# Value products moved behind the next score pair, and eight steps moved to other slots, in a two-layer attention and FFN kernel

## The chip, the cores and the metric

The kernel runs on one core of one Trainium2 chip, in one launch. The metric is the device time in microseconds, as the median of several runs. In the text TensorE (PE), VectorE (DVE), ScalarE (ACT), GpSimd (POOL) and SyncE (SP) are the engines; PEld is TensorE's weight load.

## What is computed

The input x has 16 batches of 512 tokens with 128 features, in float32. There are two layers. Each one normalizes its input (layer norm without weights) and adds an attention and an FFN, both taken from the same normalized input:

```python
xn = _layernorm(x, axis=-1)
x = x + _L0_attn_ref(xn, ...) + _L0_ffn_ref(xn, ...)
xn = _layernorm(x, axis=-1)
x = x + _L1_attn_ref(xn, ...) + _L1_ffn_ref(xn, ...)
```

Layer 0's attention has 16 heads of size 8: rotary positions, causal scores with a learned bias within 64 positions, softmax, and then `relu(probs + tau/row)`, which is nonzero in the future as well where tau is positive, and multiplies the values and Wo. Layer 0's FFN (128 to 352 and back) rounds its inputs, its hidden values and its weights to FP4 in blocks of 16. Layer 1's attention is linear and causal (elu + 1 of queries and keys, a running state of key times value, a denominator). Layer 1's FFN has four experts with a router that takes the best two, and a shared one (128 to 344 and back); the kernel computes all five for every token.

## The kernel before

A batch is handled whole, as four tiles of 128 tokens (T = 4). The work is laid out by hand in **slots**: a frame f has 64 slots (SLOTS, 16 heads times four query tiles), and in frame f slot s three batches are worked on at once. Batch f has its layer-0 scores there. Batch f+1 is being prepared at position p = s, batch f is also at position p = 64 + s (ATT = 64), batch f-1 is at p = 128 + s (L1 = 128, its layer 1), and f-2 at p = 192 + s, where the last down product ends. Frames go from -1 to 16, with 8 more slots behind. The tables of positions at the top (lines 58 to 77) say in which slot each step is issued. All engines walk through the same slots, each with its own order inside a slot; what one engine needs of another it waits for with a semaphore (lines 278 to 326). So the order on an engine is fixed by the slots, and the class Schedule (lines 96 to 151) counts the tickets of the PSUM banks in the same order.

**Scores and probabilities.** A step of four slots is one group of four heads (HG = 4) with one query tile i, whose scores have (i+1) x 128 columns. In an even slot TensorE issues the scores of this slot and the next one (`scores`, line 1073; 32 rows of float16, so one quarter of the array's rows), in two PSUM banks in turn. VectorE adds the bias and takes the maximum (`biased`, 534), ScalarE the exponential and its sum (`exp_with_sum`, 915), VectorE the reciprocal of the sums at each step's end (`row_rcp_of`, 541), GpSimd scales and adds tau in the next step (`scale_probs`, 808). Two steps after the scores, in even slots, TensorE transposes these probabilities by blocks of 128 x 128 for four heads (`turn_probs`, 1084; up to two blocks in a slot, one per turn bank), ScalarE copies them with the relu into one of four buffers pb (`store_probs`, 918), and TensorE multiplies the values by them (`pv`, 1094; weights of 32 columns, the four heads side by side in the array, 8 matmul instructions a block). Once a group's last block is done, ScalarE copies its output (`store_o`, 926).

The value products of an even slot s are issued in slot s+3 (`blocks_before`, 149), on TensorE behind the extra products and the transposes. Per frame there are 40 blocks, in 24 slots. TensorE's order in a slot is: scores of the pair, extra products into the score banks (`into_scores`, 1109), transposes, value products, and the rest (`beside`, 1235).

**Extras in the score banks** (EXTRAS, line 77; all at odd slots): fx, fv and fy are the three products for the future part of layer 0's attention (a suffix sum of xn, its values, their output), kv is layer 1's state, lin its 16 key-by-query products, tot the sum of its parts. The same two banks serve them and the scores, so each waits until VectorE has taken the last but one.

**Turn banks** (TURNS, line 75): two more banks take everything that is transposed: x, its FP4 form xq, the operand stacks of both attentions (`stack`, 1063, of queries and keys as float16 parts), the hidden values, and `intra` (1210), layer 1's products of values by lin, again with 32-column weights.

**Beside them**: `qkv` (QKV0, QKV1), gate and up products (GATE0, GATE1) with ScalarE's tanh and VectorE's two products (`silu`, 586, `hidden`, 593); the FP4 rounding of the hidden values: `hidden_amax` (671), `hidden_step` (HID_STEP, 676 and 678), GpSimd's scaling (HID_SCALED), `hidden_magic` (HID_MAGIC, 433 and 435 through `fp4_magic`), GpSimd's add, subtract and multiply; the down product of layer 0 with attention's output (WO); the norm of layer 1; the router (ROUTER, sixteen small VectorE steps, two a slot, and one exponential on ScalarE); and for each of five experts the down product (DOWN1, four slots, `down1`, 1220) and its weighted addition (`accumulate`, 651, four VectorE instructions of line 661, 667 for the shared one).

VectorE's order in a slot is: the two `biased`, the extras (`from_scores`, 548), `products`, `urgent` (norms, rope, elu), the stack's copy, the reciprocal, `beside`.

## Time and profile before

| | us |
|---|---|
| median of 3 runs | 2374.54 (2372.79 to 2376.23) |
| the profiled execution | 2369.53 |
| its span | 2367.7 |
| TensorE busy, whole span | 2128.1 (90%) |
| VectorE, ScalarE, GpSimd busy | 1642.7, 1384.6, 1157.8 |
| chain that ended last | PE 59%, DVE 19%, ACT 12%, issue 7%, POOL 2% |
| mean granted TensorE clock | 0.971 |

The busy time of TensorE is no measure of its speed: matmuls are pipelined and their ends are modelled, so that the distances between starts say more than durations. A row of the timeline merges equal neighbours: its start is that of the first, its count stands behind the x, and where two rows follow each other on TensorE, the difference of their starts is what the first one really took.

### The profile page before, as it was taken

To read this page: it belongs to the slowest core of one execution; us is meant where nothing else is said; L and a number is where in the kernel's file an instruction comes from. 1 tells how busy PE (TensorE), PEld (TensorE's weight loads), DVE (VectorE), ACT (ScalarE), POOL (GpSimd) and SP (SyncE) were. 2 spreads that over 40 slices of the span, in tenths; PEclk is the share of its full clock that TensorE was granted. 3 is DMA by queue.
4 is the path that set the end of the run, shared out by engine and by line. 5 is a ranking of instruction groups with operands and counts; after the bars stand their busy time and mean duration, and the time that the engine had idled before them with its cause. 6 is when DMAs were issued, how large, how long until landed. Compare 5 with 4: busy or idle time off the path is not lost.

```text
span 2367.7 us, 52493 instructions
## 1 busy us (share of the span) xinstructions
PE 2128.1 (90%) x18761; PEld 1371.4 (58%) x18761; DVE 1642.7 (69%) x5384; ACT 1384.6 (58%) x3797; POOL 1157.8 (49%) x1800
## 2 busy tenths in 40 slices
PE   3889989899898998989999998998989999998988
PEld 2455656656565564656656565564655656566555
DVE  7557776676777767776676766768677676765655
ACT  1766565564756656575565756656565565756642
POOL 5674553645536364463645536365463645535220
PEclk8889999999999999999999999999999999999999
DMA  4000000000000000000000000000000000000000
GB/s 121 2 6 2 10 6 2 15 2 15 2 2 15 1 15 2 6 10 2 15 2 15 2 1 15 2 15 1 1 15 2 14 2 10 1 2 10 2 10 6
DMA packets 33542, 22.03 MB, mean 9 GB/s; under 512 B 2443, under 2 KB 32771, under 8 KB 33283
## 3 DMA queue, kind: packets, MB, share of 16 engines
q1 hardware_dynamic: 33283, 18.68, 2.7%
q8 instruction: 150, 2.46, 0.4%
q14 instruction: 109, 0.89, 0.1%
HBM read 14.48 MB, written 4.19 MB: 8 GB/s over the span
## 4 chain that ended last, share of the span: by engine, by line
PE 59%; DVE 19%; ACT 12%; issue 7%; POOL 2%; DVEq 0%; ACTq 0%; POOLq 0%
PE ps L1231 8%; PE ps L1162 8%; PE ps L1091 8%; PE ps L1172 7%; PE ps L1105 5%; ACT ring L915 4%; DVE ring L534 4%; PE ps L1060 3%; PE ps L1081 3%; ACT pb L924 3%; PE ps L1216 3%; PE ps L1069 2%; PE ps L1189 2%; DVE x L661 2%; PE ps L1138 2%
## 5 line engine op out<-in xcount | busy, mean ns | idle before, releaser
L808 POOL TENSOR_SCALAR ring<-ring,row_rcp,tau_row 128x128 f32<-128x128 f32 (+3 forms) x1024 | 633.4, 626 | 911.3 <-DVE row_rcp L541 911.3
L915 ACT ACTIVATE ring<-ring,neg_max 128x128 f32<-128x128 f32 (+3 forms) x1024 | 572.1, 560 | 696.0 <-DVE neg_max L534 693.6
L1091 PE MATMUL ps<-identf,ring 128*128 128x128 f32 x2560 | 395.8, 291 | 29.1 <-ACT qkT L906 11.3
L924 ACT ACTIVATE pb<-ps 128x512 f32<-128x512 f32 x640 | 348.4, 583 | 7.9 <-PE ps L1091 7.7
L534 DVE CUSTOM_DVE_ANT_1 ring<-ps,bias_t 128x384 f32<-128x384 f32 (+1 forms) x496 | 287.1, 615 | 78.7 <-PE ps L1081 71.8
L1091 PEld LDWEIGHTS ps<-identf,ring 128*128 128x128 f32 x2560 | 281.5, 144 | 101.5 <-issue 28.0
L1231 PEld LDWEIGHTS ps<-ed_t,h 128*128 128x128 f32 (+1 forms) x1920 | 260.0, 198 | 73.2 <-issue 71.6
L534 DVE CUSTOM_DVE_ANT_0 ring<-ps,bias_t 128x128 f32<-128x128 f32 (+1 forms) x528 | 171.6, 361 | 177.8 <-PE ps L1081 176.9
L1231 PE MATMUL ps<-ed_t,h 128*128 128x128 f32 (+1 forms) x1920 | 284.4, 286 | 0.0
L1162 PE MATMUL ps<-xn1T,eg_t 128*128 128x512 f32 (+1 forms) x480 | 262.9, 630 | 22.9 <-DVE h L586 22.5
L1172 PE MATMUL ps<-xn1T,eu_t 128*128 128x512 f32 (+1 forms) x480 | 259.5, 622 | 4.0 <-ACT vx L887 3.7
L1081 PE MATMUL ps<-qkT 32*128 32x128 f16 (+3 forms) x1024 | 184.6, 310 | 54.2 <-DVE neg_max L534 35.2
L569 DVE TENSOR_TENSOR lin<-ps,tri_t 128x512 f32<-128x512 f32 x256 | 164.7, 685 | 98.5 <-PE ps L1138 95.1
L938 ACT ACTIVATE tanh_t<-ps 128x512 f32<-128x512 f32 (+2 forms) x304 | 171.7, 565 | 102.7 <-PE ps L1162 98.4
L1105 PE MATMUL ps<-pb,vx 128*32 128x128 f32 x5120 | 226.6, 284 | 3.5 <-ACT o_stack L930 3.1
L586 DVE SCALAR_TENSOR_TENSOR h<-tanh_t,ps 128x512 f32<-128x512 f32 (+1 forms) x240 | 163.4, 681 | 53.0 <-ACT tanh_t L938 53.0
L915 ACT ACTIVATION_READ_ACCUMULATOR ring<-ring,neg_max 128x1 f32 x1024 | 196.9, 192 | 0.0
L1081 PEld LDWEIGHTS ps<-qkT 32*128 32x128 f16 x1024 | 56.7, 91 | 231.8 <-issue 126.3
L1105 PEld LDWEIGHTS ps<-pb,vx 128*32 128x32 f32 x5120 | 122.3, 110 | 94.9 <-issue 67.8
L593 DVE SCALAR_TENSOR_TENSOR h<-h,ps 128x512 f32<-128x512 f32 (+1 forms) x240 | 162.7, 678 | 5.0 <-DVE x L661 3.5
L793 POOL TENSOR_TENSOR qk<-prod 128x256 f32<-128x256 f32 x128 | 96.7, 756 | 94.9 <-DVE prod L510 94.9
L783 POOL TENSOR_TENSOR hid<-hid,q_step 128x352 f32<-128x352 f32 x128 | 101.1, 791 | 9.3 <-DVE q_step L678 9.3
(161 smaller groups left out, 3235.1 us busy)
## 6 DMA issues: line engine op xcount, KB each, us to landing
x_t<-x SPq DMA_DIRECT2D x16, 256.0 KB, 2.8
x<-x SPq DMA_DIRECT2D x16, 256.0 KB, 2.8
out<-x SPq DMA_DIRECT2D x16, 256.0 KB, 2.3
bias_t<-bias SPq DMA_DIRECT2D x1, 1536.0 KB, 7.7
eg_t<-eg SPq DMA_DIRECT2D x1, 860.0 KB
eu_t<-eu SPq DMA_DIRECT2D x1, 860.0 KB
ed_t<-ed SPq DMA_DIRECT2D x2, 320.0 KB
ring<-inv_row SPq DMA_DIRECT2D x1, 256.0 KB, 2.7
```

The lines of the kernel that those rows point to most:

```text
L534: dve.tensor_tensor_reduce(out=dst, in0=src, in1=add, scale=-1.0, scalar=NO_MIN, op0=ALU.add, op1=ALU.min, accum_out=neg_max[:, n % 2, r:r ...
L569: dve.tensor_tensor(lin[:, k % NLIN, :, :], src.rearrange("p (t n) -> p t n", n=P), tri_t[:, :].unsqueeze(1).broadcast_to([P, T, P]), ALU. ...
L808: pool.tensor_scalar(e, e, row_rcp[:, m % 2, r:r + 1], tau_row[:, i, HG * g + r:HG * g + r + 1], ALU.mult, ALU.add).then_inc(p_ok.sem, 1)
L915: act.activation(e, e, ACT.Exp, bias=neg_max[:, n % 2, r:r + 1], scale=-1.0, accum_out=row_sum[:, n % 2, r:r + 1]).then_inc(exp_ok.sem, 1)
L924: act.activation(pb[:, c % NPB, :], bank(turn_bank(q)), ACT.Relu).then_inc(t_taken[q % 2].sem, 1)
L938: act.activation(tanh_t[0:rows, k % 2, 0:n], bank(G0)[0:rows, 0:n], ACT.Tanh, scale=0.5).then_inc(tanh_ok.sem, 1)
L1081: pe.matmul(o[:, 0:(i + 1) * P], qkT0[rows, g, 0, i * P:(i + 1) * P], qkT0[rows, g, 1, 0:(i + 1) * P], start=True, stop=True).then_inc(s_p ...
L1091: last = pe.transpose(o[:, r * P:(r + 1) * P], ring_of(i, r)[:, k * P:(k + 1) * P], idf)
L1105: last = pe.matmul(bank(PV)[R * r:R * (r + 1), i * P:(i + 1) * P], vx0[:, b % 2, k, v0:v0 + R], pb[:, c % NPB, r * P:(r + 1) * P], start=( ...
L1162: last = pe.matmul(bank(G0)[0:n, :], eg_t[:, e, r0:r0 + n], xn1T[:, :], start=True, stop=True)
L1172: last = pe.matmul(bank(G1)[0:n, :], eu_t[:, e, r0:r0 + n], xn1T[:, :], start=True, stop=True)
L1231: last = pe.matmul(o, h1[0:n, e % 2, c, ts], ed_t[0:n, e, c, :], start=(c == 0 and e < E), stop=(c == 2))
```

## The change

TensorE issues the value products right behind the scores of a pair, ahead of the extras and the transposes, and those of slot s come in slot s+2 in place of s+3 (`blocks_before`). ScalarE's `store_o` moves with them. The two intra products at even positions (L1 + 42 and L1 + 46) are issued right behind the value products too, and their turn tickets come before those of the transposes. The positions that change: FUTURE_X 7 to 5; the last STACK0 73 to 69; HID_STEP 22 to 36; the four of HID_MAGIC six slots earlier; FUTURE_V and FUTURE_Y four slots later; the first WO, ROUTER with its exponential, and the last DOWN1 one slot later; all accumulations one slot after the down product's last tile in place of two (for the shared expert the slot stays as it was). VectorE waits once more, for its own sum of the state.

```diff
--- before.py
+++ after.py
@@ -55,22 +55,22 @@
 ATT = SLOTS
 L1 = 2 * SLOTS
 
-TURN_X, FUTURE_X, QKV0, TURN_XQ = 5, 7, 7, 11
+TURN_X, FUTURE_X, QKV0, TURN_XQ = 5, 5, 7, 11
 GATE0 = (12, 14, 16, 18)
-STACK0 = (27, 45, 59, 73)
-HID_AMAX, HID_STEP, HID_SCALED = [p + 3 for p in GATE0], 22, (38, 39, 40, 41)
-HID_MAGIC, HID_ADD, HID_SUB, HID_MUL = (54, 56, 58, 60), (56, 58, 60, 62), (57, 59, 61, 63), (64, 66, 68, 70)
-TURN_H, FUTURE_V, FUTURE_Y = (ATT + 11, ATT + 13, ATT + 13, ATT + 15), ATT + 57, ATT + 59
-WO, WO_LAST, ADD_X1 = (L1 + 6, L1 + 8, L1 + 9, L1 + 11), L1 + 12, L1 + 14
+STACK0 = (27, 45, 59, 69)
+HID_AMAX, HID_STEP, HID_SCALED = [p + 3 for p in GATE0], 36, (38, 39, 40, 41)
+HID_MAGIC, HID_ADD, HID_SUB, HID_MUL = (48, 50, 52, 54), (56, 58, 60, 62), (57, 59, 61, 63), (64, 66, 68, 70)
+TURN_H, FUTURE_V, FUTURE_Y = (ATT + 11, ATT + 13, ATT + 13, ATT + 15), ATT + 61, ATT + 63
+WO, WO_LAST, ADD_X1 = (L1 + 7, L1 + 8, L1 + 9, L1 + 11), L1 + 12, L1 + 14
 TURN_X1, QKV1 = L1 + 19, L1 + 20
 KV, TURN_Q32 = (L1 + 29, L1 + 29, L1 + 31), L1 + 29
 STACK1 = (L1 + 31, L1 + 35, L1 + 41, L1 + 47)
 LIN = [L1 + (33, 35, 39, 41, 43, 45, 49, 51)[v // 2] for v in range(H)]
 INTRA = (L1 + 37, L1 + 42, L1 + 46, L1 + 53)
 TOT, TURN_O1 = (L1 + 55, L1 + 57, L1 + 59, L1 + 61), L1 + 63
-ROUTER = L1 + 30
+ROUTER = L1 + 31
 GATE1 = [L1 + 25 + 5 * u // 2 for u in range(3 * NE)]
-DOWN1 = [GATE1[3 * e + 2] + 4 for e in range(NE)]
+DOWN1 = [GATE1[3 * e + 2] + 4 for e in range(NE - 1)] + [L1 + 65]
 
 TURNS = (("x", (TURN_X,)), ("xq", (TURN_XQ,)), ("stack0", STACK0), ("hid", TURN_H), ("xn1", (TURN_X1,)),
          ("stack1", STACK1), ("q32", (TURN_Q32,)), ("intra", INTRA), ("o1", (TURN_O1,)))
@@ -109,13 +109,17 @@
             if self.has(f) and s % 2 == 0:
                 self.score["score", f, s] = len(self.score)
                 self.score["score", f, s + 1] = len(self.score)
+            for b, p in self.beside(f, s):
+                if p in INTRA and p % 2 == 0:
+                    self.turn["intra", b, INTRA.index(p)] = len(self.turn)
             for blk in self.blocks(f, s):
                 self.turn[("probs",) + blk] = len(self.turn)
             for b, p in self.beside(f, s):
                 for name, k in at(EXTRAS, p):
                     self.score[name, b, k] = len(self.score)
                 for name, k in at(TURNS, p):
-                    self.turn[name, b, k] = len(self.turn)
+                    if name != "intra" or p % 2:
+                        self.turn[name, b, k] = len(self.turn)
                 for layer, p0 in enumerate((QKV0, QKV1)):
                     if 0 <= p - p0 < T:
                         gate_ticket(("qkv", layer, b, p - p0), (p - p0) % 2)
@@ -148,7 +152,7 @@
 
     def blocks_before(self, f, s):
 
-        return self.blocks(f, s - 3) if s >= 3 else self.blocks(f - 1, SLOTS + s - 3)
+        return self.blocks(*divmod(SLOTS * f + s - 2, SLOTS))
 
 
 def build(nc, x, wq, wk, wv, wo, wo_pad, bias, tau, tau_col_in, wg, wu, wd, wqkv1, wout1, eg, eu, ed,
@@ -558,6 +562,8 @@
                 elif name == "fy":
                     dve.tensor_copy(y_future[0:H, :, :], src[0:H, 0:(T - 1) * D].rearrange("p (i d) -> p i d", d=D)).then_inc(s_taken.sem, 1)
                 elif name == "kv":
+                    if k >= 2:
+                        dve.wait_ge(st_ok.sem, st_ok.at(b, k - 1))
                     mask = head_mask_t[:, :, :].rearrange("p h c -> p (h c)")
                     dve.tensor_tensor(state_d[:, :] if k else state[:, 0, :], src[:, 0:H * NV], mask, ALU.mult).then_inc(s_taken.sem, 1)
                     dve.wait_ge(s_taken.sem, q + 1)
@@ -739,7 +745,7 @@
                     router(b, 2 * (p - ROUTER) + 3)
                     router(b, 2 * (p - ROUTER) + 4)
                 for e in range(NE):
-                    if p == DOWN1[e] + 5:
+                    if p == DOWN1[e] + 4:
                         accumulate(b, e)
 
             for f, s in plan.slots():
@@ -963,7 +969,7 @@
                     elu_exp(b, p - QKV1 - 3)
                 if 0 <= p - QKV1 - 5 < T:
                     stack_high(b, 1, p - QKV1 - 5)
-                if p == QKV1 + 8:
+                if p == ROUTER - 2:
                     act.wait_ge(r_ok.sem, r_ok.at(b, 2))
                     act.activation(gs[:, 0, :, :], gl[:, :, :], ACT.Exp).then_inc(rexp_ok.sem, 1)
                 if p in STACK1:
@@ -1265,7 +1271,7 @@
                 if p == TURN_Q32:
                     pe.wait_ge(elu_ok.sem, elu_ok.at(b, T))
                     turn(("q32", b, 0), lambda t: qk[:, t, 0:D])
-                if p in INTRA:
+                if p in INTRA and p % 2:
                     intra(b, INTRA.index(p))
                 if p == TURN_O1:
                     pe.wait_ge(s_taken.sem, plan.score["tot", b, T - 1] + 1)
@@ -1287,13 +1293,16 @@
                 if has(f) and s % 2 == 0:
                     scores(f, s)
                     scores(f, s + 1)
+                for blk in plan.blocks_before(f, s):
+                    pv(*blk)
+                for b, p in plan.beside(f, s):
+                    if p in INTRA and p % 2 == 0:
+                        intra(b, INTRA.index(p))
                 for b, p in plan.beside(f, s):
                     for name, k in at(EXTRAS, p):
                         into_scores(b, name, k)
                 for blk in plan.blocks(f, s):
                     turn_probs(*blk)
-                for blk in plan.blocks_before(f, s):
-                    pv(*blk)
                 for b, p in plan.beside(f, s):
                     beside(b, p)
```

## Rows read from the trace of the kernel before

**Rows 1.** windows, one whole period, then frame 0: us, busy us (instructions), clock

```profile
852.60:994.90 142.30, 130.93 (x1172) 84.54 (x1172) 101.45 (x336) 86.18 (x238) 71.92 (x113) 0.99 0.02 7
44.00:138.00 94.00, 67.15 (x551) 39.38 (x549) 58.25 (x209) 60.76 (x183) 67.12 (x101) 0.77 0.01 4
```

**Rows 2.** windows, seven stretches: slots 0-5, 6-13, 14-20, 20-27, 28-33, 34-59, 60-63

```profile
852.60:864.50 11.90, 10.39 (x88) 8.48 (x88) 8.06 (x33) 7.02 (x21) 9.19 (x15) 0.86 0.08 23
864.50:884.00 19.50, 19.50 (x170) 14.61 (x169) 8.98 (x34) 12.19 (x37) 12.57 (x19) 1.00 0.10 29
884.00:897.70 13.70, 10.37 (x80) 5.69 (x80) 10.01 (x37) 8.43 (x26) 7.37 (x13) 1.00 0.00 1
897.70:911.20 13.50, 11.33 (x93) 5.23 (x91) 13.12 (x48) 11.39 (x36) 8.13 (x15) 1.00 0.01 2
911.20:922.90 11.70, 11.09 (x76) 5.77 (x75) 10.48 (x34) 9.83 (x26) 8.12 (x14) 1.00 0.00 1
922.90:987.70 64.80, 62.40 (x633) 41.21 (x632) 44.23 (x133) 34.27 (x87) 20.31 (x32) 1.00 0.01 2
987.70:994.90 7.20, 5.85 (x48) 3.54 (x46) 6.57 (x19) 3.04 (x8) 6.22 (x8) 1.00 0.00 0
```

**Rows 3.** timeline, TensorE only: start us, us, engine, line, what

```profile
724.36 0.83 PE L1201 MATMUL ps<-wo_pad_t,o_stack 128*128 128x128 f32 x6
...
725.03 0.73 PE L1115 MATMUL ps<-suffix_t,xn 128*128 128x3 f32 x6
...
872.48 0.65 PE L1105 MATMUL ps<-pb,vx 128*32 128x128 f32 x16
...
873.06 0.94 PE L1189 MATMUL ps<-wdq,hqT 128*128 128x128 f32 x6
...
873.83 0.39 PE L1199 MATMUL ps<-y_future,tau_future 128*128 128x128 f32 x2
...
929.83 0.83 PE L1231 MATMUL ps<-ed_t,h 128*128 128x128 f32 x6
...
930.59 0.43 PE L1105 MATMUL ps<-pb,vx 128*32 128x128 f32 x8
```

**Rows 4.** timeline, TensorE: linear products and what follows them

```profile
960.24 0.41 PE L1138 MATMUL ps<-qkT 32*128 32x128 f16 x8
...
960.57 0.94 PE L1231 MATMUL ps<-ed_t,h 128*128 128x128 f32 x6
...
964.28 0.41 PE L1138 MATMUL ps<-qkT 32*128 32x128 f16 x8
...
964.62 0.64 PE L1105 MATMUL ps<-pb,vx 128*32 128x128 f32 x16
```

**Rows 5.** timeline, slot 40: scores that wait for a linear product's bank

```profile
937.72 0.33 PE L1081 MATMUL ps<-qkT 32*128 32x384 f16 x1 [0.27 <-DVE lin L569]
```

**Rows 6.** timeline, slots 23 to 27: the quantization step, TensorE's wait behind it

```profile
901.84 0.73 DVE L676 TENSOR_SCALAR q_step<-q_step 128x88 f32<-128x88 f32 x1
...
902.61 0.70 DVE L678 RECIPROCAL q_step<-q_step 128x88 f32<-128x88 f32 x1
...
909.67 1.12 PE L1162 MATMUL ps<-xn1T,eg_t 128*128 128x512 f32 x2 [1.37 <-DVE h L586]
```

**Rows 7.** timeline, slot 9: the last stack and the projection behind it

```profile
874.72 0.39 PE L1069 MATMUL ps<-ident,qx 128*128 128x128 f16 x4
...
875.17 0.86 PE L1060 MATMUL ps<-wqkv_t,xnT 128*128 128x384 f32 x2
```

**Rows 8.** timeline, waits of TensorE before scores 0 and in slot 5

```profile
721.62 0.63 PE L1048 MATMUL ps<-identf,xn 128*128 128x128 f32 x4 [1.77 <-ACT pb L924]
...
994.94 0.21 PE L1081 MATMUL ps<-qkT 32*128 32x128 f16 x1 [1.39 <-DVE neg_max L534]
```

**Rows 9.** timeline, slots 17 and 18: copies of the probabilities, scores

```profile
890.44 1.06 ACT L924 ACTIVATE pb<-ps 128x512 f32<-128x512 f32 x2
...
891.49 0.23 PE L1081 MATMUL ps<-qkT 32*128 32x128 f16 x2
```

## The prediction

> **What bounds the kernel now.** I read the windows view first, over one whole period of the steady state: one frame of 64 slots, from one batch's first score product to the next batch's. It lasts 142.3 us; TensorE is busy for 130.9, VectorE for 101.5, ScalarE for 86.2, GpSimd for 71.9 [rows 1]. Fifteen such periods hold 15 x 142.3 = 2134 us of the 2367.7 us span, so the change is decided there. Frame 0 (94 us) has TensorE busy for 67.2 us only, at a granted clock of 0.77 [rows 1]; it waits for others, and I count nothing there, nor in the start and the tail, which hold few of the steps touched.
>
> The same view in seven stretches of that period says where TensorE sets the pace [rows 2]. From slot 6 to 13 it is busy for 19.50 of 19.50 us, and from slot 34 to 59 for 62.40 of 64.80. From slot 14 to 20 it is busy for 10.37 of 13.70: a chain through ScalarE and VectorE paces it. From slot 20 to 27 VectorE is busy for 13.12 of 13.50, so VectorE is the bound. At the turn of the frame, slots 60 to 63, VectorE is busy for 6.57 of 7.20, and in slots 0 to 5 TensorE stands for 1.5 of 11.90 us at a mean granted clock of 0.86.
>
> Then I read the timeline for what a value product costs TensorE beyond its columns. Six full 128x128 products take 0.67 us from the first to the full-shape work behind them (724.36 to 725.03). Six of the same kind before value products are spaced 0.76 (929.83 to 930.59); so going to the 32-column shape costs about 0.09. Sixteen value products (two blocks) take 0.58 until the full shape starts (872.48 to 873.06); that holds another such step. The six products after them need 0.77 instead of 0.67 (873.06 to 873.83): 0.10 for starting up again. A **visit** to this shape thus costs about 0.3 us over its streaming [rows 3]. Leaving the 32-row shape costs the same whichever shape follows: eight linear products take 0.34 us to a value product and 0.33 to a full one [rows 4].
>
> **The change, part by part.**
>
> *Value products.* There are 24 slots a frame that have them (one for a step with one or two key blocks, two for one with three or four: 6 for each of four groups). Now each sits in an odd slot between full-shape work: in, out, start up, 0.3 us. Behind the scores the way is scores, value products, full, in place of scores, full: one step more, 0.1 us. Saved: 0.2 us a visit. In five slots (35, 39, 41, 43, 51) the value products stand right behind linear products and share that visit's start-up already; there one step goes and one comes: nothing. Nineteen visits x 0.2 = 3.8 us. The two intra products moved to the front of even slots (42, 46) then touch value products of the same shape and lose a whole visit each, 2 x 0.3 = 0.6 us. Together 4.4 us a frame of TensorE time.
>
> Not all of it reaches the path. Six visits (3, 5, 15, 19, 23, 63) lie where TensorE waits anyway; 13 lie in slots 7 to 11 (three), 21 to 31 (four) and 37 to 59 (six): 2.6 us, and 3.2 with the intra products. Against it: the value products of slot 39 covered part of the wait of the next scores for the linear products' bank. Even so 0.27 us of it shows [rows 5]; without the cover it grows by the products' 0.58, while later waits in slot 41 shrink. I take 0.4 off. **2.8 us.**
>
> *The quantization step* (two VectorE instructions, 0.73 and 0.70 us) leaves slot 22 for slot 36. In slots 20 to 27 VectorE has 0.4 us free in 13.5; at the end of that run TensorE waits 1.37 us for VectorE's silu [rows 2, 6]. Taking 1.43 us out should take that wait away: **1.4 us**. In slot 36 they fill idle VectorE time (44.23 of 64.80 us are busy from slot 34 to 59), and GpSimd needs the result from slot 38 on; it has 44 us free there. The bounds: nothing, if ScalarE takes over (11.39 of 13.50 us busy), and 1.4 plus about 0.4 if the waits before it shrink too.
>
> *Future products and the last operand stack.* The suffix product over x (up to 0.73 us [rows 3]) goes from slot 7 to 5, the last stack (0.45 us from its first transpose to the work behind it [rows 7]) from slot 9 to 5. They leave the stretch with TensorE busy throughout and enter slot 5, where TensorE waits for ScalarE's copy of the turned probabilities; where the clock had not dropped, that wait is 1.77 us [rows 8]. Their own time fits into it: **1.1 us**. VectorE's copy of the stack moves too, into slot 5, ahead of the turned probabilities of slot 6; the turn of x and the next scores and value products lie between, so nothing waits for it. The output product's first tile moves from slot 6 to 7, in a stretch where only the sum counts: nothing.
>
> *The turn of the frame.* The magic-number steps (two VectorE instructions each) go from slots 54 to 60 to 48 to 54, and the expert accumulation runs one slot earlier. Both relieve VectorE ahead of slot 0, where TensorE waits 1.39 us for VectorE's pass over the scores [rows 8]. But two future products with their VectorE copies come in at 61 and 63, the last between scores 63 and scores 0 in the same banks: scores 0 will wait for one more VectorE pass than now. I credit **0.6 us**, bounds nothing and 2. The magic steps' new slots have room (stretch 34 to 59). The added VectorE wait for its own state sum costs nothing: the sum is made one slot or more before. The router and the last down product go one slot later and have a slot's slack: nothing.
>
> **Sum:** 2.8 + 1.4 + 1.1 + 0.6 = 5.9 us a frame, x 15 = 88.5 us. The profiled execution took 2369.5 us (its span 2367.7 and 1.8 around it); 2369.5 - 88.5 = 2281. The median of the runs is 5.0 us above that execution: **2286 us**.
>
> **Rivals.**
>
> *The savings are absorbed* (chance 0.20). VectorE's and ScalarE's chains pace more of the frame than the four stretches (46.3 us [rows 2]) in which I saw it, and new waits stand where the old ones were. Then only visits in the two full stretches count, nine x 0.2 + 0.6 = 2.4 us, 36 us in all: 2338. For it: scores after linear products wait for VectorE in several places [rows 5]. Against it: VectorE is busy for 101.5 of 142.3 us.
>
> *More goes than counted* (0.13). With VectorE relieved at both crowded places the other waits shrink too; the stretches 14 to 27 and 60 to 5 have 8.4 us of idle TensorE time [rows 2], of which I use 3.1. With 8 us a frame: 2374.5 - 120 = 2255.
>
> *The change of shape is free* (0.02). The 0.1 us at each change could belong to what waits there, not to the shape; then the first term falls away and the shifted slots alone are left: 5.9 - 2.8 = 3.1 us a frame, 2286 + 15 x 2.8 = 2328. Against it: the rows show the same 0.1 at changes with no wait in front of them, and none between products of one shape [rows 3, 4]. The Trainium skill has such a rule: "TensorE: Matmul & The Clock Gate", Part 3 on row and column tiling, lets the load for the background weight buffer be pulled ahead of running products, charges a packed group some 4 ns a tile, and names no cost for a change of shape. The trace agrees with it within one shape only.
>
> *It does nothing measurable* (0.03). A value product now needs the copied probabilities a slot earlier. ScalarE ends the copy of slot 16 at 891.50, when the scores of slot 18 start at 891.49 [rows 9]: about 0.2 us early enough. If faster scores run into this copy in most pairs, the gain turns into waits: 2374.
>
> *Slower* (0.04). The value products (0.58 us for two blocks) now hold the transposes of the same slot back; ScalarE takes its instructions in order, copies the transposes, and only then runs the second exponential of the pair. If ScalarE becomes late by 0.35 us in each of 24 slots, 8.4 us come and 5.9 go: 2.5 x 15 = +37, 2412. It decides where the transposes end later than the first exponential; with 256 and more columns the exponential still covers them, and ScalarE has 56 us free in the period [rows 1].
>
> **Numbers.** The likeliest case (0.58) gives 2286; its own range is 2262 to 2312 (1.7 us a frame either way, from the bounds of the terms). The absorbed case adds up to 2338 and the larger one 2255, so the range is 2250 to 2342. A measurement of this kernel tells 0.2%, about 5 us, from no change. Faster by more: 0.58 + 0.20 + 0.13 + 0.02 = 0.93; same 0.03; slower 0.04.
>
> **What would show it.** The period should be near 136.4 us. Value products should start about 0.1 us behind the pair's second score product's stream, with no idle of their own; the full-shape groups in odd slots should be spaced as if undisturbed. VectorE's silu wait near slot 27 should be gone; the 1.39 us before scores 0 should be under 1; the wait of the turn of x for ScalarE should be under 0.7. It is wrong if value products wait for ScalarE's copies in many slots, if idle TensorE time in a period stays at 11.4 us or more, or if stretch 34 to 59 shortens by less than 1 us.

## The result, and the profile after

The changed kernel takes **2303.8 us** (median of 4 runs, 2302.4 to 2310.3) beside 2373.7 us of the kernel before on the same chip: ratio 0.9705, 95% interval 0.9691 to 0.9719. The forecast was 2286.0, with 2250 to 2342 as the range: the sign and the range hold, and the gain is 70 us where 88.5 were counted. The profiled execution took 2310.34 us. The first part of its page (busy us, share of the span, instructions), the TensorE clock in 40 slices, and the chain that ended last:

```profile
span 2308.5 us, 52509 instructions
PE 2078.7 (90%) x18761; PEld 1355.0 (59%) x18761; DVE 1635.0 (71%) x5384; ACT 1400.3 (61%) x3797; POOL 1147.4 (50%) x1800
PEclk7779999999999999999999999999999999999999
PE 60%; DVE 16%; ACT 13%; issue 8%; POOL 4%; DVEq 0%; ACTq 0%; POOLq 0%
```

The work is the same, the shares are nearly so; TensorE is busy for 49 us less. Where the time went is read by stretches. The windows view of one period of the changed kernel, with the columns of [rows 1] and the slots of [rows 2] (whole; slots 0 to 5; 6 to 13; 14 to 20; 21 to 27; 28 to 33; 34 to 59; 60 to 63), and frame 0:

```profile
1394.68:1532.08 137.40, 126.39 (x1174) 83.05 (x1173) 100.81 (x336) 87.17 (x239) 71.28 (x112) 1.00 0.03 7
1394.68:1405.50 10.82, 9.88 (x102) 8.38 (x102) 7.77 (x32) 6.13 (x20) 9.51 (x14) 1.00 0.09 27
1405.50:1423.22 17.72, 17.72 (x156) 13.57 (x157) 9.00 (x34) 12.03 (x35) 11.99 (x19) 1.00 0.11 31
1423.22:1436.90 13.68, 10.43 (x86) 5.74 (x86) 10.02 (x37) 8.40 (x26) 7.36 (x13) 1.00 0.01 1
1436.90:1450.80 13.90, 10.96 (x85) 5.25 (x83) 11.72 (x46) 11.78 (x36) 8.21 (x15) 1.00 0.01 3
1450.80:1461.99 11.19, 10.76 (x77) 5.89 (x75) 10.08 (x32) 9.87 (x26) 7.74 (x14) 1.00 0.00 0
1461.99:1524.79 62.80, 59.75 (x623) 39.98 (x623) 45.47 (x137) 34.63 (x87) 20.27 (x33) 1.00 0.01 2
1524.79:1532.08 7.29, 6.90 (x57) 4.24 (x55) 6.75 (x22) 4.33 (x11) 6.19 (x8) 1.00 0.00 0
42.90:145.90 103.00, 75.01 (x552) 42.85 (x550) 59.33 (x210) 63.22 (x186) 69.48 (x104) 0.68 0.01 4
```

The period is 137.4 in place of 142.3. Slots 6 to 13 lost 1.8 us and stay at full TensorE; slots 34 to 59 lost 2.0; slots 0 to 5 lost 1.1. Slots 21 to 27, where the quantization step and the visits were to bring some 2 us, are not shorter (13.90 beside 13.50), although VectorE is busy for 11.72 us in place of 13.12. Frame 0 is 9 us longer in this execution, at a clock of 0.68 in place of 0.77.

For all kernels of this study I took the starts of the scores of every pair from the trace, the median of each pair's length over frames 2 to 13, and summed them (us a frame; by slots; "runs" is the median of the timed runs):

| kernel | 60-5 | 6-13 | 14-21 | 22-33 | 34-47 | 48-59 | sum | runs |
|---|---|---|---|---|---|---|---|---|
| before | 18.96 | 19.53 | 15.82 | 23.07 | 34.68 | 30.12 | 142.2 | 2373.7 |
| order_only | 19.52 | 18.89 | 15.81 | 23.13 | 34.87 | 30.01 | 142.2 | 2379.4 |
| step_alone | 19.04 | 19.52 | 15.81 | 22.82 | 34.68 | 30.12 | 142.0 | 2368.9 |
| slots_only | 18.02 | 18.45 | 15.81 | 22.93 | 34.94 | 28.77 | 138.9 | 2319.8 |
| **after** | 18.10 | 17.72 | 15.80 | 22.98 | 34.66 | 28.14 | 137.4 | 2303.8 |
| step_back | 18.13 | 17.72 | 15.83 | 23.05 | 34.67 | 28.14 | 137.5 | 2305.8 |
| frame_start_back | 17.63 | 18.89 | 15.82 | 22.98 | 34.84 | 28.14 | 138.3 | 2311.3 |
| magic_back | 19.03 | 17.72 | 15.80 | 23.66 | 34.66 | 28.14 | 139.0 | 2325.4 |
| acc_back | 19.57 | 17.72 | 15.80 | 22.98 | 34.24 | 28.91 | 139.2 | 2335.1 |
| pv_behind_turns | 18.11 | 18.25 | 15.81 | 23.05 | 36.18 | 29.02 | 140.4 | 2345.6 |
| acc1_back | 18.10 | 17.72 | 15.80 | 22.98 | 33.36 | 28.14 | 136.1 | 2284.7 |
| old_order_acc1 | 18.04 | 18.44 | 15.83 | 22.93 | 33.75 | 28.77 | 137.8 | 2304.1 |
| pv_ahead | 18.13 | 17.72 | 15.83 | 23.00 | 32.78 | 27.57 | 135.0 | 2277.5 |
| store_late | 18.13 | 17.72 | 15.83 | 22.51 | 32.78 | 27.57 | 134.5 | **2257.4** |

Three medians in this table fall between two clocks of TensorE, since its granted clock dropped in about half of the frames: pair 26 of magic_back (5.39 us at full clock, 6.75 where it dropped; the table holds 6.07), pair 40 of pv_behind_turns (5.64 or 7.22; 6.41) and pair 40 of acc_back (6.14 or 7.04; 6.33).

### The profile page after: what moved, and what is told of

It reads as the page before. It is cut to its first block, busy times and chain, and to the rows that moved or that the text cites. A ratio compares the mean times of both kernels' runs of the same rounds, so it can differ in the third digit from the quotient of the medians.

```text
span 2308.5 us, 52509 instructions
## 1 busy us (share of the span) xinstructions
PE 2078.7 (90%) x18761; PEld 1355.0 (59%) x18761; DVE 1635.0 (71%) x5384; ACT 1400.3 (61%) x3797; POOL 1147.4 (50%) x1800
## 4 chain that ended last, share of the span: by engine, by line
PE 60%; DVE 16%; ACT 13%; issue 8%; POOL 4%; DVEq 0%; ACTq 0%; POOLq 0%
PE ps L1097 9%; PE ps L1168 9%; PE ps L1178 7%; PE ps L1237 7%; PE ps L1111 6%; ACT ring L921 4%; PE ps L1087 3%; PE ps L1066 3%; DVE ring L538 3%; ACT pb L930 3%; PE ps L1075 2%; PE ps L1222 2%; PE ps L1144 2%; PE ps L1195 2%; PE ps L1207 2%
## 5 line engine op out<-in xcount | busy, mean ns | idle before, releaser
L814 POOL TENSOR_SCALAR ring<-ring,row_rcp,tau_row 128x128 f32<-128x128 f32 (+3 forms) x1024 | 626.1, 618 | 824.4 <-DVE row_rcp L545 824.2
L1097 PE MATMUL ps<-identf,ring 128*128 128x128 f32 x2560 | 384.9, 288 | 17.9 <-ACT qkT L912 11.3
L538 DVE CUSTOM_DVE_ANT_1 ring<-ps,bias_t 128x384 f32<-128x384 f32 (+1 forms) x496 | 287.2, 615 | 82.3 <-PE ps L1087 78.3
L1097 PEld LDWEIGHTS ps<-identf,ring 128*128 128x128 f32 x2560 | 280.1, 144 | 103.8 <-issue 62.6
L1237 PEld LDWEIGHTS ps<-ed_t,h 128*128 128x128 f32 (+1 forms) x1920 | 250.7, 191 | 74.7 <-issue 73.1
L1237 PE MATMUL ps<-ed_t,h 128*128 128x128 f32 (+1 forms) x1920 | 272.3, 278 | 0.0
L1111 PE MATMUL ps<-pb,vx 128*32 128x128 f32 x5120 | 226.3, 285 | 19.0 <-ACT o_stack L936 15.9
L538 DVE CUSTOM_DVE_ANT_0 ring<-ps,bias_t 128x128 f32<-128x128 f32 (+1 forms) x528 | 172.8, 361 | 98.1 <-PE ps L1087 98.0
L1087 PE MATMUL ps<-qkT 32*128 32x128 f16 (+3 forms) x1024 | 183.3, 312 | 36.8 <-DVE lin L575 23.1
L1087 PEld LDWEIGHTS ps<-qkT 32*128 32x128 f16 x1024 | 56.2, 91 | 210.2 <-issue 92.9
L1111 PEld LDWEIGHTS ps<-pb,vx 128*32 128x32 f32 x5120 | 117.9, 110 | 81.4 <-issue 53.6
```

The source lines that it names most:

```text
L538: dve.tensor_tensor_reduce(out=dst, in0=src, in1=add, scale=-1.0, scalar=NO_MIN, op0=ALU.add, op1=ALU.min, accum_out=neg_max[:, n % 2, r:r ...
L814: pool.tensor_scalar(e, e, row_rcp[:, m % 2, r:r + 1], tau_row[:, i, HG * g + r:HG * g + r + 1], ALU.mult, ALU.add).then_inc(p_ok.sem, 1)
L1087: pe.matmul(o[:, 0:(i + 1) * P], qkT0[rows, g, 0, i * P:(i + 1) * P], qkT0[rows, g, 1, 0:(i + 1) * P], start=True, stop=True).then_inc(s_p ...
L1097: last = pe.transpose(o[:, r * P:(r + 1) * P], ring_of(i, r)[:, k * P:(k + 1) * P], idf)
L1111: last = pe.matmul(bank(PV)[R * r:R * (r + 1), i * P:(i + 1) * P], vx0[:, b % 2, k, v0:v0 + R], pb[:, c % NPB, r * P:(r + 1) * P], start=( ...
L1237: last = pe.matmul(o, h1[0:n, e % 2, c, ts], ed_t[0:n, e, c, :], start=(c == 0 and e < E), stop=(c == 2))
```

## The experiments: the order of the value products

**order_only**: the kernel before with the value products alone in their new place (the intra products stay).

```diff
     def blocks_before(self, f, s):
-        return self.blocks(f, s - 3) if s >= 3 else self.blocks(f - 1, SLOTS + s - 3)
+        return self.blocks(*divmod(SLOTS * f + s - 2, SLOTS))
...
+                for blk in plan.blocks_before(f, s):
+                    pv(*blk)
                 for b, p in plan.beside(f, s):
                     for name, k in at(EXTRAS, p):
                         into_scores(b, name, k)
                 for blk in plan.blocks(f, s):
                     turn_probs(*blk)
-                for blk in plan.blocks_before(f, s):
-                    pv(*blk)
```

> The kernel before with the new order alone (value products right behind the scores, a slot earlier; no step at another slot, intra products where they were). Shape theory: each visit to the 32-column shape loses 0.2 us on TensorE in 19 of 24 slots, and 13 of them lie where TensorE paces: 13 x 0.2 = 2.6 us a frame less 0.4 of lost cover = 2.2, x 15 = 33 us, about 2341 us. Rival, that the shape is free and only waits move: within 5 us of the kernel before, 2370 to 2378. Rival, that the earlier value products hold ScalarE back: above 2380.

Measured: 2379.35 us, ratio 1.0020 (1.0010 to 1.0029). A miss: the order alone gives nothing, and the interval even lies just above 1. The table says how. Slots 6 to 13, where TensorE never waits, lose 0.64 us for three visits, which is the 0.2 a visit of the forecast. Slots 60 to 5 take 0.56 of it back and 34 to 47 another 0.19: there TensorE waits for others, and the value products, which used to stand in the wait, now run ahead of it. In slot 5 of order_only, for one, the turn of x (the transposes of x) waits for ScalarE's copy, which comes behind VectorE's passes over the scores:

```profile
1439.21 0.63 PE L1048 MATMUL ps<-identf,xn 128*128 128x128 f32 x4 [1.12 <-ACT pb L924]
```

A saved piece of TensorE work is worth nothing at a place where it was the filling of a wait.

**slots_only**: the changed kernel with the value and intra products where the kernel before has them, so that only the moved steps are left (the reverse of the diff above, and INTRA as before).

> The changed kernel with the old order (value products three slots later, behind extras and transposes, intra products beside), so the moved steps alone. The prediction's terms for them, 1.4 + 1.1 + 0.6 = 3.1 us a frame, give 2374 - 46 = 2328. What the changed kernel's trace suggests, that the quantization step brought nothing: 1.7 x 15 = 25 us, about 2348. Rival, that the steps only help together with the new order: 2365 or more.

Measured: 2319.82 us, ratio 0.9774 (0.9760 to 0.9789). The moved steps alone bring 54 us, three quarters of the gain; on top of them the same order brings 16 us (2319.8 to 2303.8). By then the turn of the frame is cleared: there the order costs 0.08 us (18.02 to 18.10) in place of 0.56.

**pv_behind_turns**: the changed kernel with the value products in the same slot, behind the transposes.

```diff
-                for blk in plan.blocks_before(f, s):
-                    pv(*blk)
...
                 for blk in plan.blocks(f, s):
                     turn_probs(*blk)
+                for blk in plan.blocks_before(f, s):
+                    pv(*blk)
```

> The changed kernel, value products in the same slot but behind the transposes, so they stand between full-shape products again: the work, the slots and nearly the waits are the same, only the shape changes come back (in, out and start up, 0.3 us, in place of one step, 0.1) in 24 slots. Shape theory: up to 4.8 us a frame on TensorE, some 70% of it where TensorE paces: 3 to 4 us, 45 to 60 us over the changed kernel, 2350 to 2365. Rival, shape free: within 5 us of the changed kernel (2304).

Measured: 2345.61 us, ratio 0.9884 (0.9870 to 0.9899), 42 us above the changed kernel, just short of what was expected of the price of a shape change. Not all of it is that price: with pair 40 at full clock the sums differ by 2.2 us a frame, 33 us; in 6 of 12 frames the clock dropped in pair 40, which took 1.6 us more there. The 2.2 us lie in ten pairs, at 0.16 to 0.33 us each (pairs 6, 8, 34 to 40 and 50 to 56). Pairs 6 and 8 are in the stretch where TensorE is busy for 17.72 of 17.72 us, so a moved wait doesn't explain them: the rival that the change of shape is free falls. In the trace of the changed kernel a visit looks like this (timeline, TensorE, slot 22; columns start us, us, engine, line, what; a value product is at L1111, scores at L1087, transposes at L1097):

```profile
1023.23 0.28 PE L1087 MATMUL ps<-qkT 32*128 32x256 f16 x2
1023.45 0.64 PE L1111 MATMUL ps<-pb,vx 128*32 128x128 f32 x16
1024.02 1.09 PE L1097 MATMUL ps<-identf,ring 128*128 128x128 f32 x8
```

Scores, 0.22 us later value products, 0.57 us later the full shape, with no wait named on any of them: the two blocks cost what they cost before [rows 3], but only once between scores and transposes.

**old_order_acc1**: slots_only with one more edit, the old slot for expert 1's accumulation (acc1_back in the next section).

> The best kernel so far (2285: the changed kernel with expert 1's accumulation put back in its old slot), but with the value products where the kernel before has them, odd slots, behind the transposes. It tells what the order is worth once the accumulation is out of the way. If the order is worth what it was between the shifted slots alone and the whole change (16 us): 2301. If the late accumulation had hidden a part of it, more, up to my term of 2.8 us a frame, 42 us: 2327. If it is worth nothing (the order alone on the kernel before gave nothing): 2285.

Measured: 2304.08 us, ratio 0.9704 (0.9687 to 0.9720), as expected of the first theory: beside acc1_back (2284.7) the order is worth 19 us, 1.7 us a frame in the sums. By stretch: 0.72 in slots 6 to 13, 0.39 in 34 to 47, 0.63 in 48 to 59, and nothing from 14 to 33 and 60 to 5.

## The experiments: the moved steps

**step_back** (HID_STEP 36 to 22 in the changed kernel) and **step_alone** (22 to 36 in the kernel before):

```diff
-HID_AMAX, HID_STEP, HID_SCALED = [p + 3 for p in GATE0], 36, (38, 39, 40, 41)
+HID_AMAX, HID_STEP, HID_SCALED = [p + 3 for p in GATE0], 22, (38, 39, 40, 41)
```

> The changed kernel with the quantization step back at slot 22 (two VectorE instructions, 1.4 us). The prediction's term: 1.4 x 15 = +21 us, 2325. The changed kernel's trace (VectorE idles 1.2 us around slot 22 and ScalarE has no gap there): ScalarE's chain paces these slots, so VectorE's 1.4 us are mostly hidden: +0 to +6 us, 2304 to 2310.

> The kernel before with the quantization step alone moved from slot 22 to 36. My term: the wait of TensorE for VectorE's silu near slot 27 (1.37 us) goes, 1.4 us a frame, 15 x 1.4 = 21 us: 2353. Rival, from the pair-by-pair comparison of the kernels before and after: pairs 26 and 28 shorten by some 0.6 us together where the order is still the old one, 9 us: 2365. Third theory, from the kernel in which the step was put back (2 us): ScalarE's chain (stack copy, elu exponential, tanh) ends last at slot 27, the wait stays, and VectorE idles in its place: 2374 within 3 us.

Measured: 2305.8 us (ratio 0.9716, 0.9699 to 0.9732), which is the changed kernel's time, and 2368.93 us (0.9978, 0.9966 to 0.9989; 10 runs). The step is worth 0 to 6 us, not 21. The rows say why. In the changed kernel, first slot 23 (VectorE's rope product and TensorE's last projection), then the step in its new slot; below them VectorE's pass over the scores of pair 24 in step_alone:

```profile
1025.81 0.42 DVE L511 TENSOR_TENSOR prod<-ps,cos_t 128x256 f32<-128x256 f32 x1 [0.48 <-PE ps L1066]
...
1026.49 0.92 PE L1066 MATMUL ps<-wqkv_t,xn1T 128*128 128x388 f32 x2 [0.72 <-ACT vx L893]
...
1468.81 0.20 DVE L682 TENSOR_SCALAR q_step<-q_step 128x88 f32<-128x88 f32 x1
1469.04 0.70 DVE L684 RECIPROCAL q_step<-q_step 128x88 f32<-128x88 f32 x1
```

```profile
903.11 0.56 DVE L534 CUSTOM_DVE_ANT_1 ring<-ps,bias_t 128x384 f32<-128x384 f32 x1 [1.09 <-PE ps L1081]
```

The last projection waits for ScalarE's copy of a value tile out of the bank (0.72 us here, 0.52 in the kernel before and in step_alone), and the scores of pair 24 stand behind it. With the step gone VectorE only waits longer for those scores: pair 22 keeps its 3.90 us in step_alone, VectorE's idle time in it rises from 0.04 to 0.73 us, and its whole wait for the scores is 1.09. VectorE was the fullest engine of slots 20 to 27, but in their first half it was not the one that ended last.

**The silu at slot 27** stayed late as well. Timeline of the changed kernel, pairs 24 and 26 (26 starts at 1029.64), ScalarE, VectorE and TensorE:

```profile
1029.41 0.60 ACT L921 ACTIVATE ring<-ring,neg_max 128x384 f32<-128x384 f32 x1
...
1030.01 0.56 ACT L936 COPY o_stack<-ps 128x512 f32<-128x512 f32 x1
...
1030.63 0.43 ACT L948 ACTIVATE elu_m<-elu_m 128x256 f32<-128x256 f32 x1
1030.72 0.43 PE L1111 MATMUL ps<-pb,vx 128*32 128x128 f32 x8 [0.74 <-ACT o_stack L936]
...
1031.09 0.42 DVE L610 SCALAR_TENSOR_TENSOR qk<-qk,elu_m 128x256 f32<-128x256 f32 x1 [0.46 <-ACT elu_m L948]
...
1033.52 1.12 PE L1168 MATMUL ps<-xn1T,eg_t 128*128 128x512 f32 x2 [1.32 <-DVE h L592]
```

The copy of the finished output, which moved with the value products to slot 24, now runs ahead of layer 1's elu exponential; VectorE waits 0.46 us for that exponential, and the silu stands behind it in VectorE's order. At the same time the value products of slot 26 wait 0.74 us for that very copy.

**frame_start_back**: FUTURE_X back to 7 and the last STACK0 back to 73.

> The changed kernel with the suffix product over x back at slot 7 and the last operand stack back at slot 9. The prediction's term, 1.1 us of TensorE work hidden in slot 5's wait: +1.1 x 15 = +16 us over the changed kernel (2304), so about 2320. Rival, that they are not hidden in slot 5 (the changed kernel's trace shows TensorE waiting there for VectorE before the suffix product as well as for ScalarE behind the stack): 2300 to 2308.

Measured: 2311.32 us, ratio 0.9732 (0.9715 to 0.9749): 7.5 us. In the sums 1.17 us come in slots 6 to 13, 0.18 in pair 34, and 0.47 go in 60 to 5. So the two steps' own time left the full stretch as counted (0.73 + 0.45), but their new place was not free:

```profile
1540.73 0.80 PE L1121 MATMUL ps<-suffix_t,xn 128*128 128x3 f32 x6 [0.28 <-DVE neg_max L538]
...
1541.85 0.38 PE L1075 MATMUL ps<-ident,qx 128*128 128x128 f16 x4 [0.31 <-ACT pb L930]
```

The wait of 1.77 us ahead of the turn of x [rows 8] is now one of 0.28 and one of 0.31 with the two steps between, and the turn itself comes behind both.

**magic_back** (HID_MAGIC back to 54 to 60) and **acc_back** (the four routed experts' accumulations one slot later again):

```diff
-                    if p == DOWN1[e] + 4:
+                    if p == DOWN1[e] + (5 if e < NE - 1 else 4):
```

> The changed kernel with the four magic-number steps back at slots 54 to 60. The prediction gave the relieved turn of the frame 0.6 us in all, with bounds of 0 and 2. If the magic steps (1.5 us of VectorE in slot 60) are what made VectorE late at scores 0: +0.6 to +2 us a frame, 2313 to 2334. If the accumulation's move did it: 2300 to 2308.

> The changed kernel with the four experts' accumulations back two slots behind the down product's last tile (slots 39, 46, 54, 61 in place of 38, 45, 53, 60). From the traces slots 38 to 41 gained 0.7 us a frame by the earlier one (moved out of the way of the scores of slot 40) and slots 44 to 47 lost 1.2 (VectorE 2.0 us late behind the scores of slot 46). If both are the accumulation's doing and the turn of the frame gives back what it gained there: +0.7 - 1.2 + up to 1 us a frame, so -8 to +8 us, 2296 to 2312. If the accumulation has no part in the loss at slot 46: +10 to +25.

Measured: 2325.35 us (0.9793, 0.9777 to 0.9810) and 2335.09 us (0.9830, 0.9814 to 0.9847), 21 and 31 us above the changed kernel. What they have in common falls on slots 60 to 5 (0.93 and 1.47 us in the table); a part of both is the clock, whose mean was 0.970 to 0.973 and 0.964 to 0.969 in their runs, and 0.971 to 0.978 in those of the changed kernel. VectorE's additions and magic steps, in front of its passes over the scores, had made the wait of 1.39 us [rows 8]. Now scores 0 starts without one; its two products take 0.55 us, some 0.3 more than the next pair's. The second one starts 0.33 us behind the first, when VectorE's copy of the last future product is over; that is what this copy costs:

```profile
1532.08 0.55 PE L1087 MATMUL ps<-qkT 32*128 32x128 f16 x2
...
1534.47 0.23 PE L1087 MATMUL ps<-qkT 32*128 32x128 f16 x2
```

The acc_back run missed its expectation altogether, and holds two opposite halves: pair 40 gets 0.88 us longer (0.69 at full clock), pair 56 0.77, but pair 46 gets **1.30 us shorter**. Pair 46 of the changed kernel:

```profile
1491.89 1.11 DVE L667 SCALAR_TENSOR_TENSOR x<-ps,comb,x 128x128 f32<-128x128 f32 x4
...
1493.19 0.69 DVE L538 CUSTOM_DVE_ANT_1 ring<-ps,bias_t 128x512 f32<-128x512 f32 x1 [0.18 <-DVE x L667]
...
1495.15 1.13 PE L1168 MATMUL ps<-xn1T,eg_t 128*128 128x512 f32 x2 [1.11 <-DVE h L592]
```

Expert 1's four additions, which one slot later fell behind the scores' passes, now stand ahead of them, and the silu that follows holds the next gate product for 1.11 us.

**acc1_back**: only expert 1's accumulation back in its old slot.

```diff
-                    if p == DOWN1[e] + 4:
+                    if p == DOWN1[e] + (5 if e == 1 else 4):
```

> The changed kernel with expert 1's accumulation alone back at slot 46. Theory, that it is what makes VectorE 2.0 us late at the scores of slot 46: the 1.2 us lost there come back, -1.2 x 15 = -18 us, about 2286, faster than both kernels. Rival, that the loss at 46 comes from the shape of the work around it: no change, 2300 to 2308.

Measured: 2284.74 us, ratio 0.9622 (0.9608 to 0.9637), 19 us below the changed kernel; pair 46 is 4.17 in place of 5.47 us and nothing else moves. Its period, and the same spot, where the scores' pass (L538) follows the stack's copy at once:

```profile
1376.77:1512.87 136.10, 126.21 (x1174) 83.06 (x1173) 100.36 (x336) 87.18 (x239) 71.55 (x112) 1.00 0.03 7
```

```profile
1473.37 0.69 DVE L550 COPY qkT<-ps 128x1024 f16<-128x1024 f16 x1 [0.20 <-PE ps L1075]
...
1473.98 0.68 DVE L538 CUSTOM_DVE_ANT_1 ring<-ps,bias_t 128x512 f32<-128x512 f32 x1
```

## The experiments: giving the cover back

**pv_ahead**: acc1_back, with the value products ahead of the scores in the two slots where the scores wait for VectorE's copies of linear products.

```diff
+PV_AHEAD = (40, 50)
...
+                if s in PV_AHEAD:
+                    for blk in plan.blocks_before(f, s):
+                        pv(*blk)
                 if has(f) and s % 2 == 0:
                     scores(f, s)
                     scores(f, s + 1)
-                for blk in plan.blocks_before(f, s):
-                    pv(*blk)
+                if s not in PV_AHEAD:
+                    for blk in plan.blocks_before(f, s):
+                        pv(*blk)
```

> The best kernel so far (2285) with the value products of slots 40 and 50 issued ahead of the pair's scores in place of behind them. There the scores wait for VectorE's copy of a linear product (0.93 and 0.44 us in pair 40, 0.52 us in pair 50). Theory (cover): the value products of two blocks take 0.58 us and fill those waits; pair 40 falls from 5.45 by 0.5 and pair 50 from 5.48 by 0.2 to 0.4 us, one shape change of 0.1 us more is in the sum; 0.8 us a frame, 12 us: 2273. Rival: VectorE's chain sets these pairs, and its scores pass only starts later: 2285 or more.

Measured: 2277.49 us, ratio 0.9585 (0.9562 to 0.9609), 7 us below acc1_back (12 expected). The sums differ by 1.1 us a frame, which is 16 us, and the profiled execution (2267.69 us) shows all of it; the other three took 2276 to 2280 us, at a mean granted clock of 0.971 to 0.974 beside its 0.977. Slot 40 of the changed kernel, then of pv_ahead:

```profile
1475.45 0.41 PE L1144 MATMUL ps<-qkT 32*128 32x128 f16 x8
...
1476.63 0.33 PE L1087 MATMUL ps<-qkT 32*128 32x384 f16 x1 [0.77 <-DVE lin L575]
...
1477.23 0.33 PE L1087 MATMUL ps<-qkT 32*128 32x384 f16 x1 [0.26 <-DVE lin L575]
...
1477.49 0.65 PE L1111 MATMUL ps<-pb,vx 128*32 128x128 f32 x16
```

```profile
1449.06 0.41 PE L1145 MATMUL ps<-qkT 32*128 32x128 f16 x8
1449.39 0.65 PE L1112 MATMUL ps<-pb,vx 128*32 128x128 f32 x16
1450.24 0.33 PE L1088 MATMUL ps<-qkT 32*128 32x384 f16 x1 [0.20 <-DVE lin L576]
1450.83 0.33 PE L1088 MATMUL ps<-qkT 32*128 32x384 f16 x1 [0.27 <-DVE lin L576]
1451.10 0.66 PE L1098 MATMUL ps<-identf,ring 128*128 128x128 f32 x4
```

From the linear products to the scores it is 1.18 us in both; in the second the 0.6 us of value products lie inside.

**store_late**: pv_ahead, with the output copy of slot 24 behind ScalarE's value copy and elu exponential, and the value products of slot 26 behind the up product.

```diff
-PV_AHEAD = (40, 50)
+PV_AHEAD, PV_LATE = (40, 50), 26
...
+                if s == PV_LATE - 2:
+                    for b, p in plan.beside(f, s):
+                        beside(b, p)
                 for b, m, k in plan.blocks_before(f, s):
                     if STEPS[m][1] == T - 1 and k == T - 1:
                         store_o(b, STEPS[m][0])
-                for b, p in plan.beside(f, s):
-                    beside(b, p)
+                if s != PV_LATE - 2:
+                    for b, p in plan.beside(f, s):
+                        beside(b, p)
...
-                if s not in PV_AHEAD:
+                if s not in PV_AHEAD and s != PV_LATE:
...
+                if s == PV_LATE:
+                    for blk in plan.blocks_before(f, s):
+                        pv(*blk)
```

> The kernel with value products ahead of the scores in slots 40 and 50 (2277.5), and in pairs 24 and 26 two more edits: ScalarE copies a finished group's output (0.56 us) in slot 24 behind the value copy and the elu exponential, not ahead of them, and TensorE issues the value products of slot 26, which need that copy, behind the up product, where it waits 1.49 us for VectorE's silu. Theory (the copy delays the elu exponential, VectorE's next elu step waits 0.46 us for it, and the silu follows it in VectorE's order): the silu comes 0.4 to 0.5 us earlier, pair 26 falls from 5.40 to about 4.9, 7 us in all: 2271. If the value products had paced pair 26 by their own wait of 0.82 us as well, up to 1 us a frame, 2262. Rival (VectorE's own work is full here and the 0.46 us wait only moves): 2277 within 3 us.

Measured: **2257.38 us** (5 runs, 2256.2 to 2261.6), ratio 0.9513 (0.9500 to 0.9526), the fastest kernel here, 46 us below the change as made. Its period, and slots 24 to 27:

```profile
1363.69:1498.23 134.54, 125.98 (x1173) 82.93 (x1173) 100.62 (x336) 86.82 (x239) 72.04 (x113) 1.00 0.03 7
```

```profile
1415.00 0.42 ACT L949 ACTIVATE elu_m<-elu_m 128x256 f32<-128x256 f32 x1
...
1415.31 0.58 ACT L937 COPY o_stack<-ps 128x512 f32<-128x512 f32 x1
1415.45 0.43 DVE L611 SCALAR_TENSOR_TENSOR qk<-qk,elu_m 128x256 f32<-128x256 f32 x1
...
1417.89 1.12 PE L1173 MATMUL ps<-xn1T,eg_t 128*128 128x512 f32 x2 [1.25 <-DVE h L593]
```

VectorE's 0.46 us before the elu step is gone, and pair 26 falls from 5.40 to 4.91 us, as its theory said (about 4.9). The two profiled executions differ by 6.1 us (2267.7 and 2261.6), which is that theory's 7; the medians of the timed runs differ by 20. The other 13 us go with the clock: three of pv_ahead's four runs had a mean granted clock of 0.971 to 0.974 and took 9 to 12 us more than the profiled one at 0.977; four of store_late's five had 0.978 to 0.980 and took 4 to 5 us less than its profiled one at 0.975. Whether these two edits keep the clock up, or nine runs on two chips happened to fall so, stays open.

## Why the forecast was right or wrong, by its own steps

- **Right: where it is decided.** Fifteen periods carry it. The clean periods are 4.8 us shorter (142.2 to 137.4 in the table), 15 x 4.8 = 72, and 70 were measured. The agreement is not as good as it looks: the two profiled executions differ by 59 us, since frames 1 to 14 are only 4.3 us shorter on the mean (the changed kernel's clock drops, see below) and frame 0, where nothing was counted, is 9 us longer. It took 94 us before, 95 in step_alone, and 97 to 103 in one execution of each other kernel.
- **Luck in the total.** It came within 18 us although its terms did not hold. The moved steps alone were counted at 3.1 us a frame and gave 3.3 in the sums (142.2 to 138.9), but in other places: the quantization step gave 0.2 to 0.4 where 1.4 were written, slots 48 to 59 gave 1.35 where nothing was, and pair 46 took 1.2 back, which no term held. These errors cancel.
- **Value products, 2.8 us: the visit's price held, the cover was missed.** 0.2 us a visit is what slots 6 to 13 show (0.64 and 0.72 for three), and slots 34 to 59 give 1.02 where 6 x 0.2 + 0.6 - 0.4 = 1.4 were counted. The step that failed is the count of visits that lie on the path: the four in slots 21 to 31 gave nothing, since TensorE waits there too (for ScalarE's copies and for the silu). Measured: 0 on the kernel before, 16 us behind the moved steps, 19 once pair 46 is mended; 42 were written. The forecast took each term as independent of the others, and this one was not.
- **The quantization step, 1.4 us: the term that failed.** It was read from a busy share of 13.12 in 13.50 us, as if one wait at the end of a full stretch belonged to all the work in it. Measured 0 to 0.4 us a frame. The work taken out stood ahead of a point where VectorE waits for TensorE and ScalarE, and the wait of 1.37 us at slot 27 [rows 6] starts behind that point. The lower bound that was named, nothing if ScalarE takes over, is about what happened.
- **Future products and the last stack, 1.1 us:** the full stretch lost it, the turn took 0.5 back: 0.9 in the sums with pair 34, 7.5 us of 16.
- **The turn of the frame, 0.6 us: undersized.** Undoing the magic steps costs 21 us and undoing the accumulations 31, though these two can't be added, and a part of each is the clock. Of slots 48 to 59, which shortened by 1.35 us without any new order, the forecast counted nothing: it priced where the two last future products arrive, not the full stretch that they leave (acc_back accounts for 0.77 of it; the rest was not tried by itself).
- **A cost that was not in the sum:** "one slot earlier" for expert 1's additions costs 1.3 us a frame in pair 46, 19 us in all. It is a step that lands ahead of the scores' passes where TensorE's next gate product waits for what follows them. The forecast moved all accumulations in one sentence and looked only at the turn of the frame.
- **What was to be seen:** no wait before the value products (wrong in slot 26 alone, 0.74 us); the silu's wait gone (wrong, 1.32); the wait before scores 0 under 1 (right); the turn of x under 0.7 (right, 0.31 at the stack ahead of it); 34 to 59 shorter by over 1 (right, 2.0); idle TensorE time under 11.4 (just: 137.4 - 126.39 = 11.0).
- **The rivals.** The absorbed case (2338) was the right idea with the wrong place: savings were absorbed, but at 14 to 33 and by pair 46. The Trainium skill, "TensorE: Matmul & The Clock Gate", Part 3, names no cost for a change of shape. The runs show that there is one: in pv_behind_turns 0.33 and 0.19 us in the two pairs (6 and 8) of the stretch where TensorE never waits, and 2.2 us a frame in all.

## What to carry to other kernels

Before counting a saving or the move of a step, find at its own place which engine ends last, for each wait by itself: a busy share over a stretch of ten instructions or more hides that the work stands on the free side of a wait. Work that fills a wait is best left in front of what waits (value products ahead of scores that wait for a bank gave 0.6 us in each of two slots), and a copy that moves with its producer must be looked at in its own engine's order. Where a rule moves many steps at once (all accumulations one slot earlier), undo it for each one: here one of them cost 19 us, as much as the whole forecast was off.

## What the runs showed of the hardware

**The same work at two clocks.** TensorE's granted clock fell in some frames and not in others, at the same spot, behind the same work. Windows of pair 26 of the changed kernel in frames 6 and 7:

```profile
890.88:897.63 6.75, 4.68 (x25) 2.03 (x24) 4.42 (x12) 5.76 (x18) 3.85 (x7) 0.76 0.00 0
1029.64:1035.03 5.39, 3.33 (x25) 1.41 (x24) 4.42 (x12) 5.34 (x17) 3.34 (x6) 1.00 0.00 0
```

```profile
894.76 2.08 PE L1168 MATMUL ps<-xn1T,eg_t 128*128 128x512 f32 x2 [1.32 <-DVE h L592]
```

The 10 us ahead of them agree (9.12 us busy, clock 1.00, in both), and both have waits of 0.7 and 1.3 us inside; in the one the clock goes to its lower level (1.2 GHz) within the longer wait, and behind it the two gate products take 2.08 us in place of 1.12, and 1.36 us come on top. In the profiled execution of the changed kernel this happened in 6 of 14 frames at pair 26, and in three at pair 40 (1.6 us each); that is 13 us, and by such events the mean period of frames 2 to 13 is 138.3 where the clean one is 137.4. In the kernel before, the lower level came in slots 0 to 5 of 12 of the frames 2 to 15 (a mean clock of 0.84 to 0.86 there, as in [rows 2]), where TensorE waited anyway, and at pair 26 in three. The changed kernel has none in slots 0 to 5 of these frames. The same drop costs next to nothing at a place with waits to fill (periods of 142.3 to 142.7 us with it in slots 0 to 5 alone, 142.1 in the two without, in the kernel before), and 1.4 to 1.6 us at pairs 26 and 40.

**A small instruction beside GpSimd.** The first instruction of the quantization step, 128x88 in float32, took 0.73 us in slot 22 (901.84 to 902.57 [rows 6]) and takes 0.20 us in slot 36 (1468.81); the reciprocal behind it takes 0.70 in both. GpSimd's rows around the two, of the kernel before and of the changed one:

```profile
901.74 0.77 POOL L793 TENSOR_TENSOR qk<-prod 128x256 f32<-128x256 f32 x1 [0.83 <-DVE prod L510]
```

```profile
1467.12 0.45 POOL L814 TENSOR_SCALAR ring<-ring,row_rcp,tau_row 128x128 f32<-128x128 f32 x1
1469.83 0.79 POOL L789 TENSOR_TENSOR hid<-hid,q_step 128x352 f32<-128x352 f32 x1 [2.26 <-DVE q_step L684]
```

The long one ended with a GpSimd addition of 0.77 us that had started just ahead of it; beside the short one GpSimd stood idle. The other frames agree. In the kernel before, the instruction takes 0.73 or 0.74 us in the 14 batches where this addition overlaps it, and 0.20 or 0.21 in the first two, where no GpSimd instruction does. In step_alone, which moves nothing but this step, it takes 0.20 us for all 16, for one of them (at 105.04 us) beside GpSimd's scaling of the probabilities (L808). So it goes with the addition beside it and not with the slot; why the addition does it and the scaling does not, no run shows. Either way, a duration read at a crowded place need not be what the instruction costs at another.
